# A convolution, attention and mixture-of-experts block on one core: products on tiles of the array, batch in fourths

## The chip, the core and the metric

The kernel runs as one program on one NeuronCore of a Trainium2 chip, written instruction by instruction for each engine in Bass. The metric is the device time of one execution in microseconds. PE is TensorE, DVE VectorE, ACT ScalarE, POOL GpSimd and SP the engine that issues DMAs. PSUM has eight banks of 128 partitions by 512 fp32 numbers; a "product" below is one matrix multiplication instruction of the program.

## What is computed

The input x is 16 images of 64 channels and 16x16 pixels in fp32. Everything below is fp32. The reference, cut to what matters:

```python
x = group_norm(hidden_state, 32)                 # per 2 channels
x = silu(conv2d(x, w0, b0))                      # 1x1, 64 -> 64
x = group_norm(x, 16)
x = silu(conv2d(x, w1, b1, padding=1, groups=4)) # 3x3, 64 -> 128
x = group_norm(x, 2)
y = x.reshape(B, C, RADIX, Hn, 8, Wn, 8)         # four windows of 8x8 pixels, two radix halves
a = y.mean(axis=(4, 6)).max(axis=2)
a = group_norm(silu(conv2d(a, w2, b2, groups=2)), 8)
a = softmax(conv2d(a, w3, b3, groups=2) over the radix)
out = hidden_state + group_norm(einsum(y, a, weight), 32)

t = tokens(out)                                  # (16, 256, 64)
H = layer_norm(t)                                # attention runs along the 16 images, per pixel:
e = tanh(H @ fc_w.T + fc_b) @ score_w            # causal softmax over s <= t of e[s], times H[s]
t = t + causal_attend(H, e)
x = layer_norm(t)
w = softmax(mean(x, over the 16 images) @ Wr + br)   # 8 experts, weights per pixel
h = relu(bn1(x @ W1[e] + b1)); h = relu(bn2(h @ W2[e] + b2))
t = t + sum over e of (h @ Wo[e] + bo[e]) * w[e]
```

The weights of the router need the second layer norm of all 16 images, so no expert's output can be weighed before the last image has come that far.

## The kernel before

Two images lie above each other in the partitions (`x_pairs`, 64 channels each), so there are eight pairs. The pairs go through the convolutions in two halves k (four pairs each), and from the tokens on in four blocks (k, q), q being the half of the pixels. All queues follow one written table, `ORDER`: each engine goes through it and does its own part of each step. The steps that matter:

- `gn1`, `xnorm`, `gn2`, `norm0`: the two first normalisations (statistics on DVE with bn_stats and bn_aggr, a product that averages over the channels of a group, `var ** -0.5` on POOL in `power`, scaling on DVE), with the 1x1 convolution between them (L873).
- `conv.n` (`conv1`, L898): the 3x3 convolution, nine taps for each of eight blocks u = (k, j, h) of 128x512. Its fp32 operands are split: `w1hi` and `w1lo` are the rounded weights and the remainder (ACT L378, POOL L318), and `pad[h]` holds the rounded image of 64 channels in its own partitions and the remainder in the other 64 (ACT L388, DVE L587). Each tap is one product with `w1hi` and one with `w1lo`, both over 128 partitions in the reduced type fp32r. A block is finished after its nine taps and goes to `silu.u` (ACT L397) while the next block is computed.
- `ws`, `gn3`, `win`, `w2`, `gna`, `wan`, `w3`, `gate`: window means (64 bn_stats of 64 columns, L635), the second and third normalisations, the radix softmax (as a tanh) and the gate, once per half k.
- `outp` (L910, output in 64 partitions, h = 0 and 1), `gn4`, `x1`, `tok` (L915), `ln1`, `hn`, `hch`, `fc`, `score`: last normalisation, residual, tokens and scores.
- `coef`, `att`, `scan`: the causal softmax. `scan` is one tensor_tensor_scan over 512 columns (L764), for which `att` writes a transposed product (L752) and ACT spreads the decay (L446). `t2` turns the context with 8 products of 64 output rows (L964) and DVE adds it (L769); `ln2` centres the sum again with L915.
- `unit.n`, n = 0 to 31, (k, q, e, h): expert pair e (two experts in 128 partitions), layer 1 as two fp32r products (`f1hi`, `f1lo`, L1014), ReLU with scale and bias on ACT (L468), layer 2 of the unit before as one fp32 product with a block-diagonal matrix of 128 rows (L1024), ReLU on ACT (L475) into a buffer of `held`.
- `sums`, `logits`, `wt`, `wb`: the router. `mix.n`: DVE multiplies the held output by the weights (L814), PE adds it up in 64 output partitions (L1033). `finish`: DVE L822, then the store.
- `warm` and `heat` (L860, L867): 100 products of zeros that keep PE going.

```python
def layer1(n):
    ...
    for m, weights in enumerate((f1hi, f1lo)):
        ins = T.matmul(bank[Z1[n % 2]][:], weights[:, e, :], xs[:, k, q, h::2, :], start=(m == 0), stop=(m == 1))
```

Of the kernel before, what the change touches and what calls it, by code (L numbers as in the profile page):

```python
# [26 lines left out]
AX_X = mybir.AxisListType.X  # L27
# [3 lines left out]
PIX = S * S  # L31
PAIRS = B // 2
# [9 lines left out]
Q = 2  # L42
EPS = 1e-5
# [13 lines left out]
def columns(cols=COLS):  # L57
    at, out = 0, {}
    for name, n in cols.items():
        out[name] = (at, at + n)  # L60
        at += n
    return out, at


def conv_attention_experts(nc: bass.Bass, x: bass.AP, params: bass.AP, row_params: bass.AP, conv1_w: bass.AP, out: bass.AP):
# [6 lines left out]
    with ExitStack() as ctx:  # L72
# [37 lines left out]

        hch = by_block(xnorm, "p (k q n) -> p k q n")
        qch = by_block(act0, "p (k q n) -> p k q n")
        gated = by_block(norm0, "p (k q c t) -> p k q c t", c=C)
        decay = square[:].rearrange("p k q b c -> p (k q b c)").rearrange("p (k q c t) -> p k q c t", k=NK, q=Q, c=C)
# [4 lines left out]
        held = [y[:, 2 * i:2 * i + 2, :].rearrange("p b n -> p (b n)") for i in range(8)]  # L119
        held += [t[:, 2 * i:2 * i + 2, :].rearrange("p b n -> p (b n)") for t in (xin, xnorm) for i in range(4)]  # L120
        held += [more[:, i, :] for i in range(4)]
        held += [norm0[:, 2 * i:2 * i + 2, :].rearrange("p b n -> p (b n)") for i in range(4)]
        held += [t[:, k, q].rearrange("p a b -> p (a b)") for t in (ctxs, square) for k in range(NK) for q in range(Q)]


        w1raw = sb("w1raw", [P, TAPS, P])
        w1hi = sb("w1hi", [P, TAPS, P], F32R)
        w1lo = sb("w1lo", [P, TAPS, P], F32R)
        f1hi = sb("f1hi", [P, EP, P], F32R)
        f1lo = sb("f1lo", [P, EP, P], F32R)  # L130
        f2s = sb("f2s", [P, EP, P])
        w3d = sb("w3d", [C, P])
        b3d = sb("b3d", [P, 1])
        b2half = sb("b2half", [C, 1])
        wb = sb("wb", [P, Q, EP, P])
        bias_ch = sb("bias_ch", [P, Q, P])
# [21 lines left out]
        CONV1 = (2, 3)  # L158
        CHAIN = ((5, 6), (0, 1))
# [3 lines left out]
        OUT = ((0, 7), (1, 4))  # L163
# [9 lines left out]
        pool_done = sem("pool_done")  # L173
# [5 lines left out]
        pads_zeroed, consts_ready, warm_ready = sem_list("pads_zeroed", "consts_ready", "warm_ready")  # L179
        w1_hi_ready, w1_split, f1_split, weights_folded = sem_list("w1_hi_ready", "w1_split", "f1_split", "weights_folded")  # L180
        xnorm_ready, conv0_done, act0_ready, norm0_ready = sem_list("xnorm_ready", "conv0_done", "act0_ready", "norm0_ready")
        pad_hi_ready, pad_lo_ready, conv1_done, y_ready = sem_list("pad_hi_ready", "pad_lo_ready", "conv1_done", "y_ready")
        window_tanh_ready = sem("window_tanh_ready")
        gn3_shift_ready, y_normalised, gated_y_ready = sem_list("gn3_shift_ready", "y_normalised", "gated_y_ready")
        outconv_done, gn4_shift_ready, x_scaled, x1_ready = sem_list("outconv_done", "gn4_shift_ready", "x_scaled", "x1_ready")
        tok_in_psum, square_ready, hn_ready, ctx_ready = sem_list("tok_in_psum", "square_ready", "hn_ready", "ctx_ready")
        hch_in_psum, hch_ready, fc_done, qch_ready = sem_list("hch_in_psum", "hch_ready", "fc_done", "qch_ready")
        exps_in, exps_ready, coef_ready, decay_ready = sem_list("exps_in", "exps_ready", "coef_ready", "decay_ready")
        tok2_ready, centred2, square2_ready, xn2_ready = sem_list("tok2_ready", "centred2", "square2_ready", "xn2_ready")
        xsum_ready = sem("xsum_ready")  # L190
        xt_ready = sem("xt_ready")
        xs_hi, xs_ready = sem_list("xs_hi", "xs_ready")
        logits_ready, wexp_ready, wt_ready = sem_list("logits_ready", "wexp_ready", "wt_ready")
        ctx_in_psum, bias_ready, t2_biased = sem_list("ctx_in_psum", "bias_ready", "t2_biased")
        z1_done, h1_ready, z2_done = sem_list("z1_done", "h1_ready", "z2_done")
# [24 lines left out]
        ORDER = [(s.split(".")[0], int(s.split(".")[1])) for s in """  # L220
# [17 lines left out]
        def positions(names):  # L238

            found = [s for s in ORDER if s[0] in names]  # L240
            return {s: i + 1 for i, s in enumerate(found)}
# [20 lines left out]
        def halves(k, q):  # L262

            return slice(k * PK, (k + 1) * PK), slice(q * P, (q + 1) * P)
# [36 lines left out]
        def _(pool):  # L301
# [45 lines left out]
            for name, k in ORDER:  # L347
# [12 lines left out]
                elif name == "bias":  # L360
                    bias_residual()
# [802 lines left out]
```

## Time and profile before

| what | value |
|---|---|
| time, three runs | 191.03, 190.39 and 190.34 us, median 190.39 |
| profiled execution, first to last instruction | span 188.6 us (its own device time is not listed; the median is 1.8 us above the span) |
| instructions | 2259, of them PE 714 products and 714 weight loads, DVE 399, ACT 150, POOL 46 |
| PE, DVE, ACT, POOL busy | 171.2, 122.8, 90.4, 50.0 us |
| mean granted clock of PE | 0.973 |
| DMA | 4.36 MB in all |

The span is the time between the first and the last instruction. The busy time of an engine is the time in which at least one of its instructions runs; products overlap on PE, so busy time is not a sum of durations. [...] An fp32 product appears as two MATMUL and two LDWEIGHTS records.

### The profile page before, as it was taken

The page shows a single profiled execution, that of the slowest core. Times are in us where ns is not written, and L with a number is a line of the kernel's source. Part 1 is how long each engine was busy: PE and PEld are TensorE (multiplying, and loading weights), DVE is VectorE, ACT ScalarE, POOL GpSimd, SP SyncE. Part 2 cuts the span into 40 slices and gives each one's busy share as a digit, 9 for nine tenths or more (in the row PEclk, how much of TensorE's full clock was granted, in tenths as well). Part 3 has the DMA queues.
Part 4 walks back from the last instruction along what each step waited for, and adds up shares of the span by engine and source line. Part 5 has one row for each costly group of instructions (what it writes and reads, how often), then busy time and mean ns, then how long its engine had stood idle before and what let it go on. Part 6 is the DMA issues. An engine that isn't in the chain of part 4 may idle for free.

```text
span 188.6 us, 2259 instructions
## 1 busy us (share of the span) xinstructions
PE 171.2 (91%) x714; PEld 94.5 (50%) x714; DVE 122.8 (65%) x399; ACT 90.4 (48%) x150; POOL 50.0 (27%) x46
## 2 busy tenths in 40 slices
PE   7575989999999999898976899899999999999992
PEld 2132357776667466544634556376656533543220
DVE  0577996786457677589987925843513690199991
ACT  0034071161065152387106897968999945383010
POOL 8402641100320023605047630006160000093000
PEclk9858799999999999999999999999999999999999
DMA  5920000000000000000000000000000000000141
GB/s 147 414 111 0 0 2 3 0 0 0 0 0 2 0 3 0 0 2 0 3 0 2 0 0 0 0 3 0 0 0 3 0 0 0 0 0 3 45 123 56
DMA packets 3675, 4.36 MB, mean 23 GB/s; under 512 B 192, under 2 KB 3392, under 8 KB 3536
## 3 DMA queue, kind: packets, MB, share of 16 engines
q1 hardware_dynamic: 3520, 4.02, 6.1%
q10 hardware_dynamic: 144, 0.20, 0.6%
q8 instruction: 6, 0.10, 0.2%
q14 instruction: 5, 0.04, 0.1%
HBM read 3.17 MB, written 1.05 MB: 22 GB/s over the span
## 4 chain that ended last, share of the span: by engine, by line
PE 41%; DVE 27%; issue 19%; ACT 5%; POOL 4%; DMA 2%; POOLq 1%; DVEq 0%; ACTq 0%
PE bank L898 20%; PE bank L1024 4%; PE bank L915 3%; DVE xnorm L564 2%; PE bank L1033 2%; DVE norm L752 2%; DMA xin<-x 2%; PE bank L1014 2%; PE bank L860 2%; DVE ctxs L764 1%; PE bank L964 1%; DVE xnorm L814 1%; DVE y L696 1%; PE bank L855 1%; PE bank L873 1%
## 5 line engine op out<-in xcount | busy, mean ns | idle before, releaser
L1024 PE MATMUL bank<-h,f2s 128*128 128x512 f32 x64 | 33.1, 599 | 0.6 <-ACT h L468 0.5
L898 PE MATMUL bank<-pad,w1hi 128*128 128x512 f32 x72 | 32.2, 448 | 0.5 <-DVE pad L587 0.5
L898 PE MATMUL bank<-pad,w1lo 128*128 128x512 f32 x72 | 30.3, 421 | 0.0
L468 ACT ACTIVATE h<-bank,s_bnb,s_bns 128x512 f32<-128x512 f32 x32 | 24.8, 774 | 9.7 <-PE bank L1014 9.7
L860 PE MATMUL bank<-warm 128*128 128x512 bf16 x68 | 21.4, 444 | 1.3 <-POOL warm L342 1.3
L1014 PE MATMUL bank<-xs,f1hi 128*128 128x512 f32 x32 | 20.1, 628 | 0.4 <-DVE xs L778 0.4
L898 PEld LDWEIGHTS bank<-pad,w1hi 128*128 128x128 f32 x72 | 13.7, 190 | 6.7 <-issue 2.0
L898 PEld LDWEIGHTS bank<-pad,w1lo 128*128 128x128 f32 x72 | 13.7, 190 | 4.4 <-issue 0.2
L1024 PEld LDWEIGHTS bank<-h,f2s 128*128 128x128 f32 x64 | 11.6, 188 | 5.3 <-ACT h L468 2.0
L339 POOL TENSOR_TENSOR x<-x,bias_ch 128x512 f32<-128x512 f32 x4 | 6.7, 1714 | 23.9 <-DVE bias_ch L806 23.9
L1014 PE MATMUL bank<-xs,f1lo 128*128 128x512 f32 x32 | 12.6, 395 | 0.0
L397 ACT ACTIVATE y<-bank,par 128x512 f32<-128x512 f32 x8 | 5.5, 685 | 14.7 <-PE bank L898 14.5
L860 PEld LDWEIGHTS bank<-warm 128*128 128x128 bf16 x68 | 7.1, 118 | 10.6 <-issue 6.6
L635 DVE BATCH_NORM_STATS2 s_ws<-y 128x6 f32<-128x64 f32 x64 | 8.8, 209 | 3.3 <-ACT y L397 3.3
L1014 PEld LDWEIGHTS bank<-xs,f1hi 128*128 128x128 f32 x32 | 6.0, 189 | 7.9 <-issue 6.7
L915 PE MATMUL bank<-par,x 128*128 128x128 f32 x64 | 8.3, 278 | 1.5 <-DVE x L706 1.5
L915 PEld LDWEIGHTS bank<-par,x 128*128 128x128 f32 x64 | 7.9, 192 | 3.2 <-ACT x L418 2.0
L388 ACT ACTIVATE pad<-norm 64x512 fp32r<-64x512 f32 x8 | 4.8, 632 | 9.5 <-DVE norm L574 9.4
L867 PE MATMUL bank<-warm 128*128 128x512 bf16 x32 | 8.2, 380 | 0.0
L1014 PEld LDWEIGHTS bank<-xs,f1lo 128*128 128x128 f32 x32 | 6.1, 190 | 3.6 <-issue 3.6
L475 ACT ACTIVATE square<-bank,s_bnb 128x512 f32<-128x512 f32 x4 | 2.7, 687 | 10.5 <-PE bank L1024 10.4
L873 PE MATMUL bank<-xnorm,par 128*128 128x512 f32 x8 | 6.2, 894 | 1.7 <-DVE xnorm L564 1.7
(278 smaller groups left out, 311.3 us busy)
## 6 DMA issues: line engine op xcount, KB each, us to landing
par<-params SPq DMA_DIRECT2D x1, 1223.0 KB, 8.3
xin<-x SPq DMA_DIRECT2D x4, 256.0 KB, 4.4
out<-act SPq DMA_DIRECT2D x4, 256.0 KB, 2.3
w1raw<-conv_w SPq DMA_DIRECT2D x1, 576.0 KB, 5.7
par<-params ACTq DMA_DIRECT2D x1, 193.0 KB, 3.5
row_par<-row_params SPq DMA_DIRECT2D x1, 80.0 KB, 8.3
```

Source lines behind the costliest of these rows:

```text
L339: G.tensor_tensor(x1[:, pairs, pixels], x1[:, pairs, pixels], bias_ch[:, q:q + 1, :].broadcast_to([P, PK, P]), ALU.add).then_inc(t2_biased, 1)
L388: A.activation(pad[h][own, pairs, 1:S + 1, 1:S + 1], norm0[own, pairs, :].rearrange("p b (y x) -> p b y x", y=S), ACT.Copy).then_inc(pad_h ...
L397: A.activation(y[:, b:b + 3:2, :], bank[CONV1[u % 2]][:].rearrange("p (b n) -> p b n", b=2), ACT.Silu, bias=w("b1")).then_inc(y_ready, 1)
L468: A.activation(h1[n % 3][:], bank[Z1[n % 2]][:], ACT.Relu, bias=tile("bnb", P, 2 * EP)[:, e:e + 1], scale=tile("bns", P, 2 * EP)[:, e:e + ...
L635: ins = V.bn_stats(ws[:, b * WIN + n, :], img[:, n // 2, :, n % 2, :])
L860: T.matmul(bank[TURN][:], warm[:, 0:P], warm[:], start=True, stop=True)
L867: T.matmul(bank[Z1[0]][:], warm[:, 0:P], warm[:], start=True, stop=True)
L873: T.matmul(bank[CONV0[k][j]][:], w("w0"), xnorm[:, b:b + 2, :], start=True, stop=True).then_inc(conv0_done, 1)
L898: ins = T.matmul(bank[CONV1[u % 2]][:], weights[:, 3 * dy + dx, :], pad[h][:, b:b + 2, dy:dy + S, dx:dx + S], start=(dy == dx == 0 and wei ...
L915: return T.matmul(bank[CHAIN[k][q]][:, i * P:(i + 1) * P], x1[:, k * PK + i, q * P:(q + 1) * P], w("centre"), start=True, stop=True)
L1014: ins = T.matmul(bank[Z1[n % 2]][:], weights[:, e, :], xs[:, k, q, h::2, :], start=(m == 0), stop=(m == 1))
L1024: T.matmul(bank[Z2[n % 2]][:], f2s[:, e, :], h1[n % 3][:], start=True, stop=True).then_inc(z2_done, 1)
```

## The change

- **Convolution.** No split any more. There is one plain fp32 `pad`, written by DVE straight from the normalisation (L560 in the new file), and `w1` has 64 columns. For each tap of a half k there are 8 fp32 products: four groups of 32 rows (h, half), each with 64 output columns, for j = 0 and 1 with the columns exchanged. The four blocks of a half advance tap by tap together and all end with the ninth tap. `conv.n` now is tap n of 18. Output channels are laid out anew.
- **Experts.** Layers 1 and 2 are fp32 products of 64 rows and 64 columns, two per unit each, which for h = 0 and 1 take the four quarters of the array. Units are (k, e, h) over four quarters k of the batch, with all 256 pixels each. Weights are scaled with the batch norms beforehand (`s1row`, `s2row`). Ten of the first ReLUs go to DVE (`d1`, L753). PSUM banks of the output start with the bias products (`bo`) and, for quarters 1 to 3, with the transposed context (`t2`), so that `finish` is the only add.
- **Fourths.** From `ws` on everything runs four times on four images instead of twice on eight. Window sums are tensor_reduces, the squares for `gn3` come from ACT (`square_sums`, 16 activations of 256 columns).
- **Normalisations.** The products over the groups take the bn_stats output (6 numbers per image), without bn_aggr.
- **Attention.** `scan` is 30 scalar_tensor_tensors of 128x64 that continue in place, `xc` keeps the centred tokens and the context is added to it (`cen`), so nothing is centred again by PE. ACT has no decay to spread. POOL has neither the sums over the images nor the bias adds.
- **Router.** All 32 expert outputs lie in `held` until the router's weights are there, and `mix` starts after unit 23 in the table.
- **Fillers.** 23 steps (16 `warm`, 7 `heat`) of two products instead of 50.
- ACT loads its first table before the first product.

The core of the diff:

```diff
-                for dx in range(3):
-                    for weights in (w1hi, w1lo):
-                        ins = T.matmul(bank[CONV1[u % 2]][:], weights[:, 3 * dy + dx, :], pad[h][:, b:b + 2, dy:dy + S, dx:dx + S],
-                                       start=(dy == dx == 0 and weights is w1hi), stop=(dy == dx == 2 and weights is w1lo))
...
+                for j in range(2):
+                    b = k * PK + 2 * j
+                    for h in range(2):
+                        if tap == 0 and k and (j or h):
+                            pe.wait_ge(y_ready, 2 * j + h)
+                        for half in range(2):
+                            rows, at = slice(C * h + 32 * half, C * h + 32 * half + 32), C * ((half + j) % 2)
+                            ins = T.matmul(bank[CONV1[k][2 * j + h]][at:at + C, :], w1[rows, tap, :],
+                                           pad[rows, b:b + 2, dy:dy + S, dx:dx + S], start=(tap == 0), stop=(tap == TAPS - 1))
...
-                for m, weights in enumerate((f1hi, f1lo)):
-                    ins = T.matmul(bank[Z1[n % 2]][:], weights[:, e, :], xs[:, k, q, h::2, :], start=(m == 0), stop=(m == 1))
+                own = slice(h * C, (h + 1) * C)
+                for j in range(2):
+                    to = slice(j * C, (j + 1) * C)
+                    ins = T.matmul(bank[Z1[h]][to, :], f1s[own, e, to], xs[own, k], start=True, stop=True)
...
-                T.matmul(bank[Z2[n % 2]][:], f2s[:, e, :], h1[n % 3][:], start=True, stop=True).then_inc(z2_done, 1)
+                for half in range(2):
+                    rows, at = slice(half * C, (half + 1) * C), C * ((half + h) % 2)
+                    ins = T.matmul(bank[Z2[h]][at:at + C, :], f2s[rows, h, e, :], h1[n % 4][rows, :], start=True, stop=True)
+                ins.then_inc(z2_done, 1)
...
+                for t in range(BQ):
+                    if k == t == 0:
+                        continue
+                    for q in range(Q):
+                        before = ctxs[:, k, q, t - 1] if t else ctxs[:, k - 1, q, BQ - 1]
...
+                        V.scalar_tensor_tensor(ctxs[:, k, q, t], before, a_[:, q, t:t + 1], ctxs[:, k, q, t],
+                                               ALU.mult, ALU.add).then_inc(ctx_ready, 1)
...
-            warm.0 warm.1 warm.2 warm.3 warm.4 warm.5 gn1.0 warm.6 warm.7 gn1f.0 xnorm.0 gn1.1 warm.8 gn2.0 warm.9 gn1f.1 silu0.0 warm.10
+    silu0.0 warm.0 warm.1 warm.2 warm.3 warm.4 warm.5 gn1.0 silu0.1 warm.6 warm.7 gn1f.0 warm.8 warm.9 gn1.1 warm.10 xnorm.0 warm.11
```

How the instructions now stand. **On PE, from the convolution of the first half to the gate's small products** (L855 and L822 are the small products, L898 and L882 the convolution). Before, a tap is two rows, and the third product of a run of small ones (`s_wr`) comes while later blocks are still convolved:

```order
L855 MATMUL bank<-s_wr,par 64x16
L898 MATMUL bank<-pad,w1hi 128x512
L898 MATMUL bank<-pad,w1lo 128x512
...
L855 MATMUL bank<-s_wan,w3d 128x32
...
L910 MATMUL bank<-y,par 64x512 x4
```

and now:

```order
L882 MATMUL bank<-pad,w 64x512 x16
L822 MATMUL bank<-s_gn2v1raw,par 128x24
L882 MATMUL bank<-pad,w 64x512 x56
L861 MATMUL bank<-s_diag,par 128x256 x2
L882 MATMUL bank<-pad,w 64x512 x16
L822 MATMUL bank<-s_wsum,par 128x8
L882 MATMUL bank<-pad,w 64x512 x16
L822 MATMUL bank<-s_win,par 64x16
L882 MATMUL bank<-pad,w 64x512 x16
L822 MATMUL bank<-s_wr,par 64x8
```

The first half's nine taps stand in one run, and the small products of quarter 0 stand between taps of the second half.

**On DVE, at the end of the second half of the convolution** (L602 sums windows of a block whose last tap is the eighteenth, L517 is the statistics of the product `outp`):

```order
L650 TENSOR_SCALAR s_gate<-s_wt 128x128
L654 TENSOR_TENSOR y<-y,s_gate 128x1024
L627 TENSOR_SCALAR s_wh<-bank,b2half 64x16
L602 TENSOR_REDUCE s_wst<-y 128x8
L633 SCALAR_TENSOR_TENSOR s_wa<-s_wth,s_wh 64x16
...
L517 BN_STATS s_gn4v0raw<-bank 128x6 x2
```

Before, the statistics of `outp` for the first half (L548) stood ahead of the windows of blocks 6 and 7; now they stand behind those of blocks 4 and 5, which need all 18 taps.

**On PE, around the router** (L1014 and L1008 layer 1, L1024 and L1021 layer 2, L1033 the sum over the experts). Before:

```order
L995 MATMUL bank<-s_wT,row_par 128x128 x4
L1014 MATMUL bank<-xs,f1hi 128x512
L1014 MATMUL bank<-xs,f1lo 128x512
L1024 MATMUL bank<-h_1,f2s 128x512
...
L1033 MATMUL bank<-y,par 64x512 x5
```

and now:

```order
L983 MATMUL bank<-s_wT,row_par 128x128 x8
L1008 MATMUL bank<-xs,f1s 64x512 x4
L1021 MATMUL bank<-h_2,f2s 64x512 x2
L1021 MATMUL bank<-h_3,f2s 64x512 x2
L958 MATMUL bank<-par,ctxs 128x128 x4
L1032 MATMUL bank<-s_wT,row_par 128x256 x8
L1033 MATMUL bank<-more,par 64x512 x2
```

Layer 1 and layer 2 stand in groups of four products of 64 output rows, two units at a time.

## Rows read from the trace of the kernel before

**Rows 1.** The page: busy time, share of the span and count, by engine.
```profile
PE 171.2 (91%) x714; PEld 94.5 (50%) x714; DVE 122.8 (65%) x399; ACT 90.4 (48%) x150; POOL 50.0 (27%) x46
```
**Rows 2.** Busy time by stretch (length, then each engine, granted clock).
```profile
core 0: us, PE busy (x) PEld busy (x) DVE busy (x) ACT busy (x) POOL busy (x), PEclk, DMA share, GB/s
0.00:25.00 25.00, 17.79 (x46) 6.71 (x46) 15.78 (x61) 5.10 (x7) 11.51 (x13) 0.80 0.36 127
25.00:70.00 45.00, 44.85 (x179) 30.05 (x180) 31.00 (x145) 15.41 (x29) 6.72 (x5) 1.00 0.00 1
70.00:105.00 35.00, 30.08 (x191) 18.47 (x190) 27.91 (x102) 16.43 (x33) 14.50 (x12) 1.00 0.00 1
105.00:141.00 36.00, 34.51 (x155) 20.94 (x155) 18.54 (x47) 31.38 (x51) 10.56 (x14) 1.00 0.00 0
141.00:172.00 31.00, 31.00 (x108) 14.72 (x108) 16.80 (x27) 21.37 (x33) 6.73 (x4) 1.00 0.00 1
172.00:188.60 16.60, 12.96 (x40) 3.61 (x38) 12.78 (x22) 0.69 (x1) 0.00 (x0) 1.00 0.23 65
```
**Rows 3.** Chain that ended last: start, us, what; four pieces of PE.
```profile
25.05 6.43 PE bank L898 x24
...
62.10 1.87 PE bank L910 x8
...
108.51 0.86 PE bank L1024 x2
...
109.86 0.46 PE bank L1014 x2
```
**Rows 4.** L910 alone, in two short stretches: length, PE busy, PEld busy, clock.
```profile
62.02:62.10 0.08, 0.07 (x2) 0.07 (x4) 1.00 0.00 0
62.50:62.60 0.10, 0.10 (x4) 0.09 (x2) 1.00 0.00 0
```
**Rows 5.** Groups of instructions by shape, DVE: busy us, mean ns of one, idle before.
```profile
L548 DVE BATCH_NORM_STATS2 s_gn4v0raw<-bank 128x6 f32<-128x256 f32 x4 | 1.5, 422 | 1.1 <-PE bank L910 1.0
L706 DVE TENSOR_TENSOR x<-x,xin 128x256 f32<-128x256 f32 x8 | 3.3, 425 | 1.5 <-ACT x L418 1.4
L712 DVE TENSOR_REDUCE s_ln1sq<-square 128x8 f32<-128x512 f32 x4 | 2.7, 683 | 0.9 <-ACT square L429 0.9
L696 DVE TENSOR_TENSOR y<-y,s_gate 128x1024 f32<-128x1024 f32 x4 | 4.7, 1222 | 0.1
```
**Rows 6.** Timeline of DVE, two small steps of a chain: start, us, instruction.
```profile
48.84 0.17 DVE L526 TENSOR_TENSOR s_gn3v0sq<-s_gn3v0ms 128x8 f32<-128x8 f32 x1
49.04 0.17 DVE L527 SCALAR_TENSOR_TENSOR s_gn3v<-s_gn3v0ms,s_gn3v0sq 128x8 f32<-128x8 f32 x1
```
**Rows 7.** Groups by shape, POOL: the power for eight and for four images.
```profile
L314 POOL TENSOR_TENSOR s_gn3v0r<-s_gn3v,minus_half 128x8 f32<-128x8 f32 x1 | 1.6, 1635 | 15.8 <-DVE s_gn3v L527 15.8
L314 POOL TENSOR_TENSOR s_gn4v0r<-s_gn4v,minus_half 128x4 f32<-128x4 f32 x1 | 1.0, 1007 | 9.8 <-DVE s_gn4v L527 9.8
```
**Rows 8.** Groups by shape, DVE: the first scaling for k = 1 and k = 0.
```profile
L564 DVE TENSOR_SCALAR xnorm<-xin,s_gn1v1r,s_gn1v1nb 128x256 f32<-128x256 f32 x4 | 3.8, 1009 | 0.0
L564 DVE TENSOR_SCALAR xnorm<-xin,s_gn1v0r,s_gn1v0nb 128x256 f32<-128x256 f32 x4 | 1.4, 409 | 0.0
```
**Rows 9.** Groups by shape: ReLU of layer 2, and two pieces of the attention.
```profile
L475 ACT ACTIVATE y<-bank,s_bnb 128x512 f32<-128x512 f32 x8 | 5.5, 684 | 0.1
L752 DVE TENSOR_TENSOR norm<-hn,s_coefb 128x512 f32<-128x512 f32 x4 | 4.2, 1040 | 0.0
L757 DVE SCALAR_TENSOR_TENSOR norm<-ctxs,s_coefa,norm 128x64 f32<-128x64 f32 x2 | 0.7, 350 | 0.1
```
**Rows 10.** Chain that ended last, at the end: start, us, what.
```profile
175.08 1.80 DVE xnorm L814 x3
...
182.07 3.17 PE bank L1033 x11
185.26 0.69 DVE act L822
```
**Rows 11.** Busy time in one stretch of the start, columns as in rows 2.
```profile
10.00:15.00 5.00, 4.50 (x8) 1.85 (x8) 3.50 (x16) 2.33 (x3) 0.00 (x0) 0.54 0.15 59
```

More of the change, by code:

```diff
@@ L42 @@
 Q = 2
+STRIP = 32
+NQ = 4
+STRIPS = NQ
+PQ = PAIRS // NQ
+BQ = B // NQ
 EPS = 1e-5
@@ L120, in conv_attention_experts @@
[L120 to L128, printed above, removed]
@@ L236, in conv_attention_experts, with positions @@
-        """.split()]
-        def positions(names):
-            found = [s for s in ORDER if s[0] in names]
+        def positions(names, without=()):
+            found = [s for s in ORDER if s[0] in names and s not in without]
             return {s: i + 1 for i, s in enumerate(found)}
-        SMALL_AT = positions({"gn1", "gn2", "s2row", "gn3", "w2", "gna", "w3", "gn4", "score", "sums", "logits", "wt", "wb", "bias"})
-        STATS_AT = positions({"gn1", "gn2", "gn3", "w2", "gna", "w3", "gn4"})
+        SMALL_AT = positions({"gn1", "gn2", "s1row", "s2row", "gn3", "w2", "gna", "w3", "gn4", "score", "logits", "wt", "wb"}, {("wb", 1)})
@@ new lines, in spread_first_scales @@
+            def spread_first_scales():
+                act.wait_ge(scales_folded, 1)
+                for v in range(2):
+                    for e in range(EP):
+                        A.activation(spread1[:, v, e, :], w("ident"), ACT.Copy,
+                                     scale=tile("bns", P, 3 * EP)[:, v * EP + e:v * EP + e + 1]).then_inc(spread1_ready, 1)
+            def relu1(n):
+                m, h = n // 2, n % 2
+                if (m, h) not in ON_DVE:
+                    act.wait_ge(z1_done, n + 1)
+                    if m >= 2:
+                        act.wait_ge(z2_done, n - 3)
+                    col = h * EP + units[n][1]
+                    A.activation(h1[n % 4][:], bank[Z1[h]][:], ACT.Relu, bias=tile("bnb", P, 3 * EP)[:, col:col + 1]).then_inc(h1_ready, 1)
@@ new lines, in attend @@
+            def attend(k):
+                t0, t1 = k * BQ, (k + 1) * BQ
+                dve.wait_ge(exps_ready, k + 1)
+                ex = tile(f"aexp{k}", P, 2, Q, BQ)
+                inv, b_, a_ = (tile(f"{part}{k}", P, Q, BQ) for part in ("inv", "coefb", "coefa"))
+                for q in range(Q):
+                    ins = V.tensor_tensor_scan(runsum[:, q, t0 + 1:t1 + 1], ex[:, 0, q], ex[:, 1, q], runsum[:, q, t0:t0 + 1], ALU.mult, ALU.add)
+                step(ins)
+                V.tensor_tensor(a_, ex[:, 0], runsum[:, :, t0:t1], ALU.mult)
+                step(V.reciprocal(inv, runsum[:, :, t0 + 1:t1 + 1]))
```

1000 lines of the change are left out of this document (479 added, 521 removed).

## The prediction

> **What bounds the kernel now.** I read the page's busy times first, then busy time by stretch, then the chain that ended last, then the groups by shape for prices. PE is busy for 171 of 188.6 us and DVE for 123 [rows 1]. By stretch [rows 2] this has four parts. Up to 25 us the first two normalisations run as a chain, with PE waiting and filling. From 25 to 70 PE is busy 44.85 of 45: the 3x3 convolution sets the pace. From 70 to 105 DVE is at 27.9 of 35, the highest share it reaches, and the chain goes from one small DVE step to the next. From 105 to 172 PE is full again (65.5 of 67) with the experts, ACT next to it (31.4 of 36 in the first half). The last 16.6 us are a tail of DVE weighing outputs and PE adding them. So a change to PE's work counts twice, in the convolution and in the experts, and what stays between them is DVE's.
>
> **Price of a product.** In the chain 24 fp32r products of the convolution take 6.43 us, 0.268 each, a plain fp32 product of 128 rows and 512 columns 0.86, and the split pair of layer 1 0.46 [rows 3]. The convolution is 144 such fp32r products, some 38 us with the small ones between them. The new one is 144 whole fp32 products of 32 rows and 64 columns. One after the other they would cost 144 x 0.86 = 124 us, so all hangs on overlap. The chain shows overlap for two tiles [rows 3]: the four products of L910, 64 output columns each, take 1.87 us, 0.47 each instead of 0.86. [...] Nothing in this trace has two products in different rows at once. Bounds for one tap (8 products): 8 x 0.43 = 3.44 us if only two overlap, 8 x 0.86 / 8 = 0.86 if all eight do. I take 0.86, since the row nearest to it shows tiles that pass each other freely. Then the 144 products last 144 x 0.86 / 8 = 15.5 us instead of 38.
>
> [...]
>
> **The start, to the first tap.** Before, it comes at 25.05 [rows 3]. Gone are, in each of three statistics on the way, bn_aggr and some copies, five small steps net of which a part overlaps (at [rows 6], 0.7 for each statistic, 2.1), the split of the padded image after the normalisation (an ACT and a DVE step of 512 columns, 1.4), and ACT's table load in front of the first activation. The scaling of k = 1 took 3.8 us against 1.4 for k = 0 [rows 8], while POOL worked on the split of the weights; that work is gone, 2.4 us. Those sum to 5.9 and the table load, of which I count 4.5, since the table now begins the statistics of k = 1 (1.6 us) ahead of the scaling of k = 0 and the clock is at its low level for most of 10 to 15 us [rows 11], where new fillers do not help the 0.86 product. First tap at 20.5.
>
> **To the first gate.** The nine taps of the first half end at 28.6. Its four blocks come out together, so ACT needs 3 x 0.69 for three SiLUs and four squares of 256 columns (0.5 each, an estimate from L475's 0.684 for 512 columns [rows 9]) before quarter 0 can be normalised: 32.7. The chain gn3 to gate has 18 small DVE steps of 0.20 [rows 6], two powers of 1.0 instead of 1.64 us [rows 7], four small products of 0.5 with their hand-overs and two tanhs: 9.5 us, to 42.2. The taps of the second half stand between these products on PE and end at the same time, since the chain takes longer than their 8 us. Each small product waits for DVE with taps queued behind it, but those taps have slack: their y is taken up by DVE only behind the gate.
>
> **To the first layer 1: DVE.** From the first tap to the first ReLU of the experts DVE issues, by count of the new order: 136 small steps x 0.20 = 27.2 [rows 6]; 12 memsets and the weight steps, 3; 12 bn_stats x 0.42 = 5.0 and 8 residual steps x 0.43 = 3.4 [rows 5]; 4 padded scalings, 1.4 [rows 8]; four gates x 1.4 = 5.6 [rows 5]; 22 steps of 512 columns x 0.67 = 14.7 [rows 5]; 14 steps of the scan. These are 128x64, of which [rows 9] have 0.35 with a stride of eight; 0.17 is the small step, and with contiguous columns I take 0.23, so 3.2. Sum 63.5 us. Up to the gate DVE is idle for 6.6 of 21.7 us, so 48 remain after 42.2. At 85% (rows 2 have 80% in the same stage, now there are four quarters to choose from instead of two halves) they take 56.5 us: the first ReLU comes at **99**, against about 105 before [rows 2]. So the 22 us that PE saves in the convolution arrive here as 6 us, because DVE cannot follow: that stage gets more small steps (four chains for two), which the shorter powers and the cheap scan barely pay for.
>
> **Experts to the router.** From 99 to the router's logits: DVE 10 ReLUs, 16 scan steps, the attention of two quarters and three second layer norms, 27 us. ACT 12 + 18 ReLUs x 0.69 and 6.5 of copies, 27. PE 10 groups of layer 1 and 9 of layer 2, four products on four tiles for 0.86: 16.5, plus 5 of transposes and scores and 3 for changes between tile shapes, 25. Three engines alike in load, and a chain of 14 us for the last quarter inside. At 80%: 34 us, to **133**. Before, 105 to 141 did half of the units and the attention of one half at 0.86 + 0.46 for each unit.
>
> **Router to the end.** PE: 5.5 + 7 groups x 0.86 = 10.8; 32 sums x 0.43 = 13.8; bias, spread weights and context 4; shape changes 1: 29.6. DVE: 4.5 for the router, 32 x 0.60 = 19.2 for weighing (three in 1.80 [rows 10]) and 2.4 for finishing: 26. ACT has 18 and is covered; if ACT fell behind, PE's layer 2 and then the sums would wait for it. PE sets it: 162.6. Then the last finish 0.69 and the store, which takes 188.6 - 185.95 = 2.65 behind it [rows 10]: **166.0** span. The profiled span is 188.6 and the median 190.39, so I add 1.8: **168 us**.
>
> Costed at nothing: the DVE step L752 of 1.04 [rows 9] is now contiguous, counted at 0.67; 54 fillers fewer after the first tap (68 before, 14 now by the tables) stood where PE waited anyway or cost it little; larger weight DMAs (row parameters four times) land long before their use; POOL loses its adds and sums, and nobody waits for it there any more.
>
> **Rivals.**
> *Only two tiles overlap* (the bound of 3.44 per tap). For it: no row shows different rows at once. [...] The first half would end at 51.5, the second at 82.5. DVE has the windows of blocks 4 and 5 ahead of almost everything else, so it stands until 83, has 46 us left at 85%, and the first ReLU comes at 137. Layers 1 and 2 are 128 products x 0.43 = 55 on PE, with 14 for the sums and 10 for the rest 79: 216, and 221 us in time. Slower. It decides from where a tap takes more than about 2.4 us: 22 us over the forecast are gone when the second half ends at 64.
> *Four tiles overlap, not eight*: 1.72 per tap, second half at 51.5, the rest as in the forecast, 9 us later: 177.
> *PE's clock falls* between 42 and 99. PE has some 4.5 us of real work per quarter there and only 7 filling steps, so it is busy a third of the time; at the start it was at 0.54 with 4.5 of 5 us busy, after idle time [rows 11]. Each quarter's chain gets up to 4.5 us longer, partly beside another quarter's: 7 more, 175.
> *DVE and ACT interleave better* than before, 92% instead of 85 and 80: first ReLU at 94, router at 123, end at 150, time 154.
>
> **Numbers.** Forecast case 0.45, its own range 160 to 175. Clock falls 0.17, four tiles 0.08, better interleaving 0.16, two tiles 0.12. The remaining 0.02 is a mixture that ends near the old time. All but the two-tile case and that rest are faster: 0.86 faster, 0.01 within 0.5% (1 us, what a measurement of this kernel tells apart), 0.13 slower. The range from 153 to 186 leaves out the two-tile case and the ends of the others.
>
> **What would show it.** Right: eight convolution products in 0.9 to 1.1 us; first tap near 20.5; y of blocks 4 to 7 at 42 to 45; DVE over 80% busy between 45 and 95; four expert products in 0.9; first layer 1 near 99; DVE weighing in a row from 138. Wrong: taps of over 1.7 us; a granted clock of 0.5 between 45 and 95; a first layer 1 product before 92 or after 106; ACT or PE waiting in a row behind `h1` in the expert stage.

## The result, and the profile after

| | before | after |
|---|---|---|
| median of four runs (lowest to highest), us | 190.37 (189.65 to 191.03) | 140.68 (140.55 to 141.96) |
| ratio, 95% interval | | 0.741 (0.7374 to 0.7447) |
| span of the profiled execution, us | 188.6 | 139.0 |

The change takes a quarter off the time. The forecast was 168.0 us with a range of 153 to 186: the direction held, the size did not, and the true time lies below the range. The profiled spans differ by 49.6 us, the medians by 49.7, so the two traces hold the whole difference. Medians in the experiments are of fast runs: six single runs more than 1.5% above the fastest of their kernel (one each of c3, c4, c6 and d2, two of d1) are left out.

The page after, busy time by engine, which answers to [rows 1]:

```profile
PE 120.3 (87%) x891; PEld 52.6 (38%) x891; DVE 110.3 (79%) x379; ACT 79.8 (57%) x172; POOL 33.8 (24%) x34
```

Busy time by stretch, cut where the stages now end: first tap, first gate, first layer 1, last product ahead of the router's, end. Columns as in [rows 2]:

```profile
0.00:18.20 18.20, 14.66 (x46) 5.41 (x47) 10.89 (x44) 3.75 (x6) 6.26 (x12) 1.00 0.62 206
18.20:38.60 20.40, 19.77 (x296) 8.30 (x304) 13.52 (x70) 10.62 (x35) 6.25 (x5) 1.00 0.01 2
38.60:77.10 38.50, 28.45 (x154) 16.68 (x139) 36.26 (x142) 25.45 (x64) 14.79 (x13) 0.87 0.00 1
77.10:105.70 28.60, 27.39 (x197) 11.73 (x198) 26.08 (x79) 22.92 (x40) 6.51 (x4) 1.00 0.00 1
105.70:139.00 33.30, 30.05 (x209) 10.49 (x206) 23.51 (x46) 17.06 (x30) 0.00 (x0) 1.00 0.09 33
```

PE lost 51 us of busy time, DVE 12.5. PE is no longer full from the first tap to the end: between 38.6 and 77.1 DVE is, at 36.26 of 38.50. Behind that PE sets the pace again (27.39 of 28.60), with DVE at 26.08.

The chain that ended last, after (start, us, what):

```profile
18.21 1.98 PE bank L882 x32
20.52 6.18 PE bank L882 x110
...
36.20 1.90 PE bank L882 x32
38.94 1.23 DVE y L654
...
77.11 1.09 PE bank L1008 x8
...
106.38 1.02 PE bank L1021 x8
107.40 0.86 PE bank L1008 x8
...
128.73 7.07 PE bank L1033 x32
135.82 0.69 DVE act L790
```

The 144 fp32 products of the convolution (8 for each of 18 taps) stand in the trace as 288 MATMUL and 288 LDWEIGHTS records (L882 below), two of each for a product, so 16 MATMUL records are one tap: 32 in 1.98 us are two taps at 0.99, and 110 in 6.18 are 0.90 a tap. Eight records of layers 1 and 2 are a group of four products on four tiles, 1.02 us behind another shape and 0.86 behind the same one. The groups say the same from the other side (line, busy us, mean ns of one; the convolution's 18.1 us are 1.01 a tap over all 18):

```profile
L1008 PE MATMUL bank<-xs,f1s 64*64 64x512 f32 x128 | 19.6, 608 | 2.0 <-ACT h L446 1.2
L1021 PE MATMUL bank<-h,f2s 64*64 64x512 f32 x128 | 20.1, 604 | 0.0
L882 PE MATMUL bank<-pad,w 32*64 32x512 f32 x288 | 18.1, 598 | 0.3 <-DVE pad L560 0.3
L882 PEld LDWEIGHTS bank<-pad,w 32*64 32x64 f32 x288 | 6.1, 130 | 7.4 <-issue 6.7
```

A record still lasts 0.6 us, yet 288 of them fit into 18.1. Short stretches of the convolution alone (length, PE busy, PEld busy, clock) show how:

```profile
20.60:20.65 0.05, 0.05 (x8) 0.05 (x12) 1.00 0.00 0
20.80:20.90 0.10, 0.10 (x8) 0.00 (x0) 1.00 0.00 0
20.90:21.00 0.10, 0.10 (x16) 0.07 (x8) 1.00 0.00 0
```

Eight records are under way at once, as many as there are tiles, and the next eight start only behind 20.9. For comparison one product of 128x128 without another of its line beside it, in the kernel **before** (timeline of PE: start, us, instruction):

```profile
108.35 1.02 PE L1024 MATMUL bank<-h,f2s 128*128 128x512 f32 x2
```

Its two records take 1.02 us in all and 0.59 each, so they start 0.43 apart.

By stage: the first tap comes at 18.2 instead of 25.05 (6.8 earlier); from there to the first layer 1 (77.1, before 105.3) it takes 58.9 us instead of 80.3 (21.4 less); from there to the end 61.9 instead of 83.3 (21.4 less).

### The profile page after: what moved, and what is told of

It is laid out like the page before. It is cut to its first block, busy times and chain, and to the rows that moved or that the text cites. A ratio compares the mean times of both kernels' runs of the same rounds, so it can differ in the third digit from the quotient of the medians.

```text
span 139.0 us, 2634 instructions
## 1 busy us (share of the span) xinstructions
PE 120.3 (87%) x891; PEld 52.6 (38%) x891; DVE 110.3 (79%) x379; ACT 79.8 (57%) x172; POOL 33.8 (24%) x34
## 4 chain that ended last, share of the span: by engine, by line
PE 58%; DVE 31%; issue 4%; ACT 4%; POOL 2%; DVEq 0%; ACTq 0%; POOLq 0%
PE bank L1021 12%; PE bank L1008 12%; PE bank L1033 10%; PE bank L882 7%; PE bank L830 5%; DVE s_wst L602 4%; DVE y L654 3%; DVE hn L681 2%; DVE x L668 2%; PE bank L822 2%; PE bank L943 2%; DVE s_ln1sq L675 1%; ACT y L387 1%; PE bank L935 1%; PE bank L843 1%
## 5 line engine op out<-in xcount | busy, mean ns | idle before, releaser
L1008 PE MATMUL bank<-xs,f1s 64*64 64x512 f32 x128 | 19.6, 608 | 2.0 <-ACT h L446 1.2
L1021 PE MATMUL bank<-h,f2s 64*64 64x512 f32 x128 | 20.1, 604 | 0.0
L882 PE MATMUL bank<-pad,w 32*64 32x512 f32 x288 | 18.1, 598 | 0.3 <-DVE pad L560 0.3
L446 ACT ACTIVATE h<-bank,s_bnb 128x512 f32<-128x512 f32 x22 | 14.4, 687 | 5.0 <-PE bank L1008 5.0
L830 PE MATMUL bank<-warm 128*128 128x512 bf16 x32 | 10.3, 473 | 1.3 <-POOL warm L333 1.3
L882 PEld LDWEIGHTS bank<-pad,w 32*64 32x64 f32 x288 | 6.1, 130 | 7.4 <-issue 6.7
L1008 PEld LDWEIGHTS bank<-xs,f1s 64*64 64x64 f32 x128 | 5.2, 131 | 9.7 <-ACT h L446 4.8
L753 DVE TENSOR_SCALAR h<-bank,s_bnb 128x512 f32<-128x512 f32 x10 | 7.5, 746 | 1.4 <-PE bank L1008 1.4
L1021 PEld LDWEIGHTS bank<-h,f2s 64*64 64x64 f32 x128 | 5.5, 132 | 7.9 <-issue 3.9
L602 DVE TENSOR_REDUCE s_wst<-y 128x8 f32<-128x512 f32 x8 | 5.4, 676 | 1.9 <-ACT y L366 1.9
L374 ACT ACTIVATE more<-y 128x256 f32<-128x256 f32 x16 | 6.5, 413 | 0.0
L720 DVE SCALAR_TENSOR_TENSOR ctxs<-ctxs,s_coefa 128x64 f32<-128x64 f32 x30 | 6.2, 278 | 0.1
L517 DVE BATCH_NORM_STATS2 s_gn1v0raw<-xin 128x6 f32<-128x256 f32 x4 | 1.4, 414 | 4.9 <-DMA xin<-x 4.9
```

The costliest lines, as they stand in the source:

```text
L374: A.activation(more[:, u, i * PIX:(i + 1) * PIX], y[:, 2 * u + i, :], ACT.Square, accum_out=tile(f"wsum{k}", P, 2, BQ)[:, 1, s + i:s + i + ...
L446: A.activation(h1[n % 4][:], bank[Z1[h]][:], ACT.Relu, bias=tile("bnb", P, 3 * EP)[:, col:col + 1]).then_inc(h1_ready, 1)
L602: ins = V.tensor_reduce(tile(f"wst{u // 2}", P, BQ * WIN)[:, s * WIN:(s + 2) * WIN], y[:, 2 * u:2 * u + 2, :].rearrange("p s (a y c x) -> ...
L720: V.scalar_tensor_tensor(ctxs[:, k, q, t], before, a_[:, q, t:t + 1], ctxs[:, k, q, t], ALU.mult, ALU.add).then_inc(ctx_ready, 1)
L753: V.tensor_scalar(h1[(2 * m + 1) % 4][:], bank[Z1[1]][:], tile("bnb", P, 3 * EP)[:, col:col + 1], 0.0, ALU.add, ALU.max).then_inc(h1_by_dv ...
L830: T.matmul(bank[TURN][:], warm[:, 0:P], warm[:], start=True, stop=True)
```

## The experiments

Unless it says otherwise a kernel is the one after with one edit, and + or - is against its 140.68 us.

### How many tiles overlap: c1_conv4 and c2_conv2

The order of the convolution's products alone is changed, so that four or two of its eight tiles follow each other, not all eight.

```diff
-                for j in range(2):
...
-                    for h in range(2):
...
-                        for half in range(2):
...
+                products = [(j, h, tap, half) for j in range(2) for tap in range(TAPS) for h in range(2) for half in range(2)]    # c1
+                products = [(j, h, tap, half) for j in range(2) for h in range(2) for tap in range(TAPS) for half in range(2)]    # c2
+                for j, h, tap, half in products[8 * part:8 * part + 8]:
```

> The changed kernel with the 72 convolution products of a half in the order j, tap, h, half, so that only four tiles are in use at a time. Theory 'all tiles overlap': eight products take 1.7 us instead of 0.9, a half lasts 15.5 us instead of 8; blocks 0 and 1 come no later, blocks 4 to 7 some 3 to 10 us later, DVE fills part of it: time +3 to +8 us over 140.7. Theory 'the convolution has nothing to do with it, DVE is full anyway': within 1 us.

> The same in the order j, h, tap, half: two tiles in use at a time. Theory 'all tiles overlap, so the order of products sets the rate': eight products take 3.44 us, the second half's last block comes near 80 us instead of 38, and the time rises by 30 to 40 us, to the 175 of the old kernel's class. If two tiles of different rows did not overlap at all, 6.9 us for eight and a time over 230 us.

Measured: c1 152.33 us (+11.7), c2 177.61 (+37). The convolution's group in c1, then in c2:

```profile
L880 PE MATMUL bank<-pad,w 32*64 32x512 f32 x288 | 30.1, 593 | 0.3 <-DVE pad L560 0.3
```

```profile
L880 PE MATMUL bank<-pad,w 32*64 32x512 f32 x288 | 55.0, 592 | 0.2 <-DVE pad L560 0.2
```

The same 288 records of the same shape take 18.1, 30.1 and 55.0 us with eight, four and two tiles next to each other: 1.01, 1.67 and 3.06 us for eight products. The order is what the overlap hangs on. In c2 these 3.06 are a mean over places where one block follows another; its first 16 products, all of one block, take 3.54 for eight (start, us, what):

```profile
17.99 7.09 PE bank L880 x32
```

c1 came out 4 us above what was expected of it: nearly all of the 12.0 us that its convolution is longer arrives. Its chain lies on PE, with the small products between the taps, from 17.97 to 50.77, where the chain after leaves PE at 26.7 for most of the time up to 36.2; the first layer 1 comes at 88.2 instead of 77.1.

### Layer 2 and layer 1: c3_l2full, c8_l1rows, b1_l2tiles

c3 makes layer 2 one product of 128x128 (half of it zeros, built by POOL), c8 makes layer 1 one product of 64x128 for each unit.

```diff
-                for half in range(2):
-                    rows, at = slice(half * C, (half + 1) * C), C * ((half + h) % 2)
-                    ins = T.matmul(bank[Z2[h]][at:at + C, :], f2s[rows, h, e, :], h1[n % 4][rows, :], start=True, stop=True)
+                T.matmul(bank[Z2[h]][:], f2b[:, h, e, :], h1[n % 4][:], start=True, stop=True).then_inc(z2_done, 1)
```

```diff
-                for j in range(2):
-                    to = slice(j * C, (j + 1) * C)
-                    ins = T.matmul(bank[Z1[h]][to, :], f1s[own, e, to], xs[own, k], start=True, stop=True)
+                T.matmul(bank[Z1[h]][:], f1s[own, e, :], xs[own, k], start=True, stop=True).then_inc(z1_done, 1)
```

> The changed kernel with layer 2 as one product of 128 rows and 128 columns with a half empty matrix, which POOL puts together from the scaled weights. PE does 0.86 us for each of 32 units instead of 0.43. Theory 'PE is full from the first layer 1 to the end': +10 to +14 us. Rival 'DVE or ACT sets the expert stage as much': under +6 us.

> The changed kernel with layer 1 as one product of 64 rows and 128 columns per unit instead of two of 64 columns. Theory 'only the share of the array counts': two units still take 0.86 us, time within 0.5 us. Rival 'a change of tile shape costs about 0.1 us each time': +2 to +4 us, since layer 1 and 2 now differ in shape.

Measured: c3 152.58 us (+11.9), c8 141.89 (+1.2). Layer 2 in c3 (the profiled execution took 154.81):

```profile
L1030 PE MATMUL bank<-h,f2b 128*128 128x512 f32 x64 | 32.3, 628 | 0.0
```

32.3 us against 20.1, 12.2 more, and the time rises by 11.9. That agrees with PE as the engine that sets the stage from 77 us on. For layer 1 the cut into columns is worth little: two units in different rows already overlap (1.06 us for the four records of both, below, where one full product took 0.86 [rows 3]), and what c8 loses is 1.2 us. In c8 the two layers differ in shape, and no group of either takes less than 1.02 in its chain:

```profile
120.88 1.06 PE bank L1006 x4
121.94 1.02 PE bank L1018 x8
```

b1 asks the opposite on the kernel **before**: only its layer 2 is cut into two diagonal products of 64x64.

```diff
-                T.matmul(bank[Z2[n % 2]][:], f2s[:, e, :], h1[n % 3][:], start=True, stop=True).then_inc(z2_done, 1)
+                for half in range(2):
+                    own = slice(half * C, (half + 1) * C)
+                    ins = T.matmul(bank[Z2[n % 2]][own, :], f2s[own, e, own], h1[n % 3][own, :], start=True, stop=True)
```

> The kernel before with layer 2 as two products of 64 rows and 64 columns on the diagonal, everything else as it was. Theory 'tiles of different rows and columns overlap and PE is full in the expert stage': 0.43 us less for each of 32 units, -9 to -13.8 us from 190.4. Rival 'the gain needs the new order and fourths': under 4 us.

Measured: 196.54 us (195.76 to 196.99), ratio to before 1.0329 (1.0281 to 1.0378): **slower** by 6 us. The expectation had the wrong sign. The chain of b1, one unit of layer 2 at a time:

```profile
107.99 1.01 PE bank L1026 x4
...
110.05 1.00 PE bank L1026 x4
```

One full product took 0.86 [rows 3], the two small ones take 1.01 together. They do overlap, else their four records would take some 1.72 (an estimate from the 0.43 of L1024), but a group of four small ones takes 0.86 as well, as long as one full product, so a pair of them gains nothing over the full product that does both their work, and each change between tile shapes adds about 0.15 (1.01 less 0.86). The split pair of layer 1 behind them takes 0.66 in six pieces of this chain (0.67 in one of the chain before), against 0.46 in [rows 3]. In the new order products of *two units* stand next to each other and fill all four tiles; the cut alone, in the old order, loses.

### The first 18 us: b2_splitdve

The kernel **before**, with POOL's part of the weights' split given to DVE.

```diff
                 elif name == "w1":
-                    split_w1()
...
+            def low_w1():
+                dve.wait_ge(w1_hi_ready, 1)
+                V.tensor_tensor(w1lo[:], w1raw[:], w1hi[:].bitcast(F32), ALU.subtract).then_inc(w1_split, 1)
```

> The kernel before with the split of the convolution weights on DVE (one step of 1152 columns, 1.2 us) instead of POOL. Theory 'POOL's split slowed the scaling of the second half from 1.4 to 3.8 us': first tap 1 to 2 us earlier and the time down by as much. Rival 'the scaling was slow for another reason': first tap 1.2 us later.

Measured: 189.29 us against 190.64 in the same rounds, ratio to before 0.9929 (0.9903 to 0.9954), 0.9 to 1.8 us faster. In its trace:

```profile
L562 DVE TENSOR_SCALAR xnorm<-xin,s_gn1v1r,s_gn1v1nb 128x256 f32<-128x256 f32 x4 | 1.4, 407 | 0.0
L567 DVE TENSOR_TENSOR w1lo<-w1raw,w1hi 128x1152 fp32r<-128x1152 f32 x1 | 1.4, 1351 | 0.0
```

The scaling of k = 1 falls from the mean of 1009 ns of [rows 8] to 407 once POOL's subtraction is gone, and DVE pays 1.35 us for it: 2.4 less 1.4 leaves 1 us, and the first tap comes at 24.14 instead of 25.05. The mean of 1009 hides what happened before: three of the four scalings took 0.40 us as ever, and one stood through the whole of POOL's step (the kernel **before**, timelines of DVE and POOL):

```profile
19.40 2.82 DVE L564 TENSOR_SCALAR xnorm<-xin,s_gn1v1r,s_gn1v1nb 128x256 f32<-128x256 f32 x1
```

```profile
19.46 2.61 POOL L318 TENSOR_TENSOR w1lo<-w1raw,w1hi 128x1152 fp32r<-128x1152 f32 x1
```

After the change both are gone, and L546 takes 410 ns apiece for k = 1.

### The granted clock: c4_noheat and c5_moreheat

c4 leaves out the seven filling steps of the order, c5 puts in six more between 40 and 48 us. The edit of c5:

```diff
-    outp.0 gna.1 ws.5 gnaf.1 silu.6 silu.7 gn3.2 gn4.0 gn3f.2 ynorm.1 wan.1 gn4f.0 ws.6 w3.1 win.2 ws.7 w2.2 gn3.3 heat.0 gna.2 tok.0
+    outp.0 heat.7 gna.1 ws.5 gnaf.1 silu.6 silu.7 gn3.2 heat.8 gn4.0 heat.9 gn3f.2 ynorm.1 wan.1 gn4f.0 ws.6 heat.10 w3.1 heat.11 win.2 ws.7 w2.2 heat.12 gn3.3 heat.0 gna.2 tok.0
```

> The changed kernel without the seven filling steps behind the convolution. [...] Theory 'DVE sets the pace there and PE has slack': within 1.5 us of 140.7, up or down. Rival 'the clock matters': +3 us or more.

> The changed kernel with six more filling steps of two products between the small products behind the convolution (40 to 48 us). Theory 'the low clock of 43 to 53 us costs something': it goes away and the time falls by 0.5 to 2 us. Rival 'DVE is full, the clock is free': within 0.5 us, or slower by up to 2 us, as the fillers stand in front of products that DVE waits for.

Measured: c4 143.38 us (142.97 to 144.15), +2.7; c5 140.96, no difference. After, the clock, given as a share of the full one, falls once, while PE is little used (columns as above):

```profile
40.00:45.00 5.00, 2.17 (x10) 1.19 (x10) 4.53 (x22) 5.00 (x17) 1.08 (x2) 0.91 0.02 5
45.00:50.00 5.00, 2.82 (x11) 1.63 (x10) 4.57 (x24) 4.40 (x17) 1.99 (x3) 0.50 0.00 0
50.00:55.00 5.00, 4.76 (x18) 3.13 (x18) 4.72 (x15) 3.53 (x9) 3.09 (x3) 0.57 0.01 2
```

That is 0.50 of the full clock, behind a stretch in which PE was busy 2.17 of 5 us. In c5 the mean granted clock is 1.0, with the same time, and its first layer 1 comes at 76.6 instead of 77.1: there DVE sets the pace and PE's slower products hide beside it. What the new fillers themselves cost is not told apart from what the clock gives back.

In c4 the clock is low more often, 0.76 in the mean from 55 to 95 us, against 1.00 after. The execution that was profiled is the longest of its runs (146.47 us, span 144.6), so it shows where the time goes and not how much the median has of it. One stretch and two pieces of its chain:

```profile
60.00:65.00 5.00, 5.00 (x20) 3.33 (x21) 3.88 (x13) 2.02 (x6) 1.76 (x3) 0.66 0.00 0
```

```profile
80.64 1.98 PE bank L1008 x8
...
91.06 1.02 PE bank L1008 x8
```

Of the 5.6 us by which this span is longer, 3.5 have come up before the first layer 1 (80.6 instead of 77.1) and 2.1 behind it. From 60 to 65 us PE is full and DVE is busy 3.88 us, where the kernel after has 4.89; at 80.6 a group of layer 1 takes 1.98 us at a clock of 0.50, where it takes 1.02 at 91.06 with 1.00, and PE is what that stage waits for. So the low clock happens after the change, as a rival had it, and costs nothing that shows at 45 to 55 us, where DVE stays busy; in c4 it comes also where DVE runs out of work behind PE, and among the experts. The seven fillers of the change are worth 2.7 us.

### What DVE's time is worth: c6_dveload, d3_loadheat, c7_reluact

c6 adds eight additions of 512 columns whose output nobody reads, two behind the first layer norm's statistics of each quarter; d3 is c6 with c5's fillers. c7 gives the ten first ReLUs that DVE has to ACT.

```diff
+                if name == "ln1":
+                    for i in range(2):
+                        V.tensor_tensor(tile(f"idle{i}", P, 512), w("ffn1"), w("ffn2"), ALU.add)
```

> The changed kernel with two adds of 512 columns on DVE, needed by nothing, behind each of the four statistics of the first layer norm: eight adds x 0.65 = 5.2 us, six of them ahead of the first layer 1. Theory 'DVE has no slack between 40 and 78 us': +4 to +5.5 us. Rival 'the chains have slack': under +2.

> The eight idle DVE additions of 512 columns (c6, +6.1 us) together with the six further fillers at 40 to 48 us (c5, no change). Theory (c6 is DVE's 8 x 0.67 = 5.4 us, and its remaining 0.7 the low clock that it had in places where c5 has none): +5.4, 146.1, granted clock over 0.95. Rival (c6's whole excess is DVE's, the clock costs nothing while DVE sets the pace): +6.1, 146.8.

> The changed kernel with all first ReLUs on ACT: DVE does 7.5 us less in the expert stage, ACT 6.9 more. Theory 'PE is full there and DVE was a little late': between -1 and +4 us; ACT's share in 77 to 106 us goes from 80% to nearly 100%, so I expect +3.

Measured: c6 146.46 us (145.56 to 147.03; +5.8), d3 147.23 (146.59 to 148.1; +6.6), c7 141.25 (+0.6). The additions take 0.69 each in the traces, 5.5 us for eight, and that arrives in full. But only six of them, 4.1 us, stand ahead of the first layer 1, and it comes at 82.5 in c6 and 82.1 in d3 instead of 77.1. d3 has the full clock from 45 to 55 us where c6 has it at 0.54, and is no faster, so that fall costs nothing under load either. What comes on top of the additions is open: both traces show a granted clock of 0.83 in the mean from 55 to 95 us, where the kernel after has 1.00, and no run took that away. c7 takes 7.5 us of work from DVE and gains nothing: from 77.1 to 105.7 DVE falls to 19.49 us, while ACT goes from 22.92 to 26.98 of 28.60 and PE stays near full (27.39, in c7 27.90).

### The price of a small DVE step: d1_smallfree and d2_smallchain

Twelve additions of 16 columns behind the same statistics, 48 in all, in d1 without a wait, in d2 each with a wait for its own end.

```diff
+                    for i in range(12):
+                        V.tensor_tensor(tile(f"idle{i}", P, 16), w("ffn1")[:, 0:16], w("ffn2")[:, 0:16], ALU.add)           # d1
+                        step(V.tensor_tensor(tile(f"idle{i}", P, 16), w("ffn1")[:, 0:16], w("ffn2")[:, 0:16], ALU.add))     # d2
```

> The kernel after with 48 small DVE additions (128 rows, 16 columns, nobody uses their output), twelve behind the first layer norm's statistics of each quarter, none waiting for another. Theory (independent small steps cost about 0.07 us, start to start, and the stretch from the first tap to the first expert is DVE's): 48 x 0.07 = 3.4 us, of which c6 says all arrives: +3 to +4, 144.2. Rival (a small step costs 0.20 whatever stands next to it, as the prediction priced it): +9.6, 150. Rival (the stretch has idle places on DVE that take small steps): under +1.

> The same 48 small additions, each followed by a wait for its own end before the next. Theory: 0.20 us each, +9.6 less what a wait frees: +8 to +10, 149.5; the difference to the run without waits, 48 x 0.13 = 6 us, is the error of the price in the prediction. Rival (the price is the same with and without the wait): within 1 us of that run.

Measured: d1 145.5 us (two runs, 144.73 and 146.2; +4.8), d2 153.1 (152.37 to 153.2; +12.4). The twelve as one row of DVE's timeline (start, us, instruction), in d1 and in d2:

```profile
53.44 1.13 DVE L679 TENSOR_TENSOR s_idle<-par 128x16 f32<-128x16 f32 x12
```

```profile
53.44 2.51 DVE L679 TENSOR_TENSOR s_idle<-par 128x16 f32<-128x16 f32 x12
```

0.09 us a step against 0.21, less than half; that is 5.5 us for 48. The two medians differ by 7.6 us. Above what the steps occupy (4 x 1.13 = 4.5 and 4 x 2.51 = 10.0) d1 lies by 0.3 us and d2 by 2.4. As in c6 this rest wasn't taken apart; the granted clock from 55 to 95 us is 0.96 in d1's trace and 0.78 in d2's. The kernel after has both prices next to each other on DVE:

```profile
44.20 0.17 DVE L520 SCALAR_TENSOR_TENSOR s_gn4v0raw<-s_gn4v0raw 128x4 f32<-128x4 f32 x1
44.28 0.16 DVE L495 COPY s_gn3v2ms<-bank 128x8 f32<-128x8 f32 x1
44.48 0.16 DVE L497 SCALAR_TENSOR_TENSOR s_gn3v2sq<-s_gn3v2ms 128x4 f32<-128x4 f32 x1
44.67 0.16 DVE L498 SCALAR_TENSOR_TENSOR s_gn3v<-s_gn3v2ms,s_gn3v2sq 128x4 f32<-128x4 f32 x1
44.75 0.16 DVE L641 TENSOR_TENSOR s_wan<-s_wa,s_gnav1ms 64x16 f32<-64x16 f32 x1
```

A step that belongs to another chain starts 0.08 us behind the one before it, while that one, 0.16 long, still runs; a step that needs the one before it starts 0.19 or 0.20 behind. Of the four distances here two are of each kind. The trace of the kernel **before** has them too:

```profile
82.12 0.17 DVE L746 TENSOR_TENSOR s_coefa<-s_aexp,s_runsum 128x8 f32<-128x8 f32 x1
82.21 0.20 DVE L747 RECIPROCAL s_inv<-s_runsum 128x8 f32<-128x8 f32 x1
82.44 0.17 DVE L748 TENSOR_TENSOR s_coefb<-s_aexp,s_inv 128x8 f32<-128x8 f32 x1
82.52 0.16 DVE L749 TENSOR_TENSOR s_coefa<-s_coefa,s_inv 128x8 f32<-128x8 f32 x1
```

The first and the third distance from start to start is 0.09 and 0.08 (L747 doesn't need L746, nor L749 L748), the second 0.23. From 70 to 105 us 24 of the 56 small steps that stand by themselves in DVE's timeline before are followed within 0.13 us, and the mean of all 68 is 0.14; from 38.6 to 77.1 after it is 41 of 91, and 0.15 for all 99.

## Why the prediction was right and wrong

**Price of a product: right.** Forecast 0.86 for a tap, shown 0.90 to 0.99 in the chain and 1.01 over all 18; forecast 0.86 for a group of four, shown 0.86, and 1.02 behind another shape. The two rivals on overlap are excluded by the kernel itself, and c1 and c2 show that their prices were near: 1.67 where the text had 1.72, and 3.06 (3.54 within one block) where it had 3.44. That all eight tiles overlap was the author's estimate: [rows 3] have 0.47 us for each product of L910 on two tiles, and no row before has products in different rows at once. The two records of one product of L1024 start 0.43 us apart, so the two MATMULs that run within the first 0.08 us of [rows 4] are of two products, and the rows at 20.60 have eight records under way at once.

**The start: right in kind, 2.3 us short.** Forecast 20.5, shown 18.2. Of the 5.9 us counted, 4.5 were booked, because the clock was expected low as in [rows 11] (0.54); in the stretch up to 18.2 the granted clock is now 1.00, and the gain is 6.8. b2 confirms the 2.4 us for the scaling.

**To the first gate: right.** Forecast 42.2 for it, shown 38.94 to 40.17, earlier by little more than the 2.3 us of the start. DVE was idle 20.40 - 13.52 = 6.9 us of this, forecast 6.6.

**To the first layer 1: the step that failed.** The forecast had the first ReLU on DVE at 99; it starts at 78.7. Of these 20.3 us 2.3 are the start. The forecast put 78.5 us between the first tap and this ReLU, 63.5 of steps and 15.1 of idle time (6.6 up to the gate, 8.5 behind it, by its 85%). Shown are 60.5. The steps are priced here as the forecast priced them, from the start of one to the start of the next (after's timeline of DVE, without six waits of 0.37 to 1.91 us).

The big steps came out as put: the 22 of 512 columns 14.9 (14.7), twelve bn_stats 4.5 (5.0), the gates 5.6 (5.6), residual and padded scaling 4.7 (4.8), the scan 2.7 (3.2). The small steps, the memsets and the weights took 22.8 us, against 27.2 + 3. **The term "136 small steps x 0.20" is mis-sized**: it took the distance of two steps of one chain for the price of all. Counted with the gates' four, the 143 small steps take 22.2 us, 0.155 each: 52 are followed within 0.13 us, 0.08 in the mean, most others after 0.20. d1 and d2 show this difference by itself. With the other steps the sum is 55.1 instead of 63.5, 8.4 us less. The lower price is no gift of the four quarters: before, the mean was 0.14 in the stage from 70 to 105 us, so it could have been counted there.

The rest, 9.7 us, is the second wrong step: **"at 85%"**. The six waits make 5.4 us in all, and all come before the first gate; behind it there is none, where 8.5 were forecast, and from 38.6 to 77.1 DVE is busy for 94% (36.26 of 38.50), the remaining 2.2 us being the gaps inside chains that the 0.20 already has in it. The value was taken from the kernel before, whose 80% came from two halves that often both waited. That four quarters instead of two halves fill these waits is the likely reading; no run varies the number of quarters alone.

**Experts to the router: work nearly right, density wrong.** Forecast 27 us for DVE and ACT each, 25 for PE, at 80% 34 us. Shown from 78.7 to the router's logits at 106.4: 27.7, in which DVE is busy 24.5, ACT 23.1 and PE 26.5. In the window 77.1 to 105.7 PE is at 96%, DVE at 91%. c3 agrees with PE as the one that sets it (12.2 us more work, 11.9 more time). Six more us of the miss.

**Router to the end: right.** Forecast 33 us, shown 139.0 - 106.4 = 32.6; the last finish takes 0.69 as put.

Together: 20.3 + 6.3 + 0.4 = 27.0 us, which is 166.0 - 139.0. The rival "DVE and ACT interleave better" had the density (92%) but the price of 0.20 for every small step, and so stopped at 154. Even that left 27 us from the router to the end, where the forecast's own sum has 29.6 of PE's work and then 3.3: with these it would have been 158. The rival "PE's clock falls" happened from 44 us on (0.50 from 45 to 50), and c5, with 1.00 from 45 to 55 us and the same time, shows it without effect there.

The prediction priced groups of four products and did not ask what the cut is worth without the new order: b1 shows that alone it makes the old kernel slower. No run takes the fourths, the new scan or the new normalisations out by themselves, so their shares of the gain are not shown.

## What to carry to other kernels

Price a small step twice, once behind a step that it needs (0.20 us here) and once behind one that it doesn't (0.08), and count in the trace of the kernel at hand how many are of each kind: 0.14 was the mean before, and 0.15 after. Don't carry the idle share of the old kernel over to an order with more independent pieces: the 80% before became 94%. Cut a product into tiles only if the order then puts enough independent products next to each other to fill the array, since a full group of four lasts as long as one whole product (0.86 us here). And ask of a fall in the clock, or of an added step, whether another engine waits for the slowed one: the fall at 45 us cost nothing that shows, while the seven fillers, without which it was 0.76 in the mean from 55 to 95 us instead of 1.00, were worth 2.7 us (c4).

## What was not expected of the hardware

- With all eight tiles of 32 rows by 64 columns in use, fp32 products of 512 columns reach 0.90 us for eight (in a run of seven taps), close to eightfold (0.86 for one of 128 rows), though each has two MATMUL records, which in one product of L1024 by itself start 0.43 us apart.
- A change of tile shape costs about 0.15 us (1.02 against 0.86 in the chain after, 1.01 in b1, 1.02 and 1.06 for every group in c8).
- A small DVE step that needs nothing of the one before it starts 0.08 to 0.09 us behind it, while that one, 0.16 long, still runs; one that needs it starts 0.20 behind (d1, d2 and both timelines).
- ACT's squares with a running sum bring an instruction of their own to read the sum (groups of the kernel after), 199 ns beside the 413 of the square, half as much again:

```profile
L374 ACT ACTIVATE more<-y 128x256 f32<-128x256 f32 x16 | 6.5, 413 | 0.0
L374 ACT ACTIVATION_READ_ACCUMULATOR more<-y 128x1 f32 x16 | 3.2, 199 | 0.0
```

- POOL's subtraction of 1152 columns (2.61 us) does not slow DVE's scalings evenly: it holds up one of them, 2.82 us instead of 0.41, and the ones before and behind it take 0.40. Without it none is held up (b2).
